# Router logits of an expert layer in four column tiles, summed by the matmuls that turn them

## The reference, cut to what matters

```python
x = hidden_states.reshape(-1, D)                     # 4096 x 512, after a layer norm
scores = jax.nn.softmax(x @ router_w, axis=-1)       # router_w is 512 x 8
topk_w, topk_idx = jax.lax.top_k(scores, TOP_K)      # 6 of 8 experts
g = jnp.einsum('td,edf->etf', x, w_gate)
u = jnp.einsum('td,edf->etf', x, w_up)
f_all = jnp.einsum('etf,efd->ted', jax.nn.silu(g) * u, w_down)
```

## Time and profile before

| | us |
|---|---|
| median of 3 executions | 2532.1 |
| fastest and slowest | 2517.46, 2537.41 |
| the profiled execution | 2517.62 |
| its span, first to last instruction | 2515.8 |
| mean granted TensorE clock, share of full | 0.973 |
| busy: TensorE matmuls, VectorE, ScalarE, GpSimd | 2391.5, 1376.7, 1181.9, 1334.4 |
| the logits' matmuls, L2354, busy | 22.8 + 7.5 |
| the transposes, L2362, busy | 2.6 |

### The profile page before, as it was taken

One profiled execution on the slowest core, in us unless ns is written; L12 is line 12 of the kernel. 1 busy time (PEld: TensorE's weight loads), 2 busy tenths in 40 slices (PEclk: granted clock), 3 DMA queues, 4 the chain that ended last, 5 costly groups with the idle time before them and its releaser, 6 DMA issues.

```text
span 2515.8 us, 34809 instructions
## 1 busy us (share of the span) xinstructions
PE 2391.5 (95%) x12552; PEld 1788.2 (71%) x12552; DVE 1376.7 (55%) x2160; ACT 1181.9 (47%) x2321; POOL 1334.4 (53%) x1415
## 2 busy tenths in 40 slices
PE   7999998999996999999789999999999999999998
PEld 6888884566665455554468877888777887788887
DVE  5555445777763455554554447544475444755544
ACT  3555566776731333333244435444354443544442
POOL 1444453433321122223477767777677776777773
PEclk9999997999996899999889999999999999999999
DMA  7655446666627344452322111321113211131120
GB/s 198 169 129 142 124 107 162 194 188 178 178 101 177 89 112 119 144 153 83 130 59 84 51 51 51 117 84 51 51 51 118 84 51 51 51 117 51 57 61 34
DMA packets 173963, 264.25 MB, mean 105 GB/s; under 512 B 13312, under 2 KB 100096, under 8 KB 165504
## 3 DMA queue, kind: packets, MB, share of 16 engines
q1 hardware_dynamic: 173536, 261.77, 36.7%
q10 hardware_dynamic: 256, 0.26, 0.0%
HBM read 167.55 MB, written 67.11 MB: 93 GB/s over the span
## 4 chain that ended last, share of the span: by engine, by line
PE 47%; DVE 2%; issue 1%; ACT 0%; POOL 0%; DVEq 0%; ACTq 0%
PE ex_pg L2381 30%; PE ex_pd L2397 17%; PE ex_pd L2354 1%; DVE ex_xb L2202 0%; DVE stage L2198 0%; DVE ex_ht L2231 0%; DVE ex_up L2222 0%; DVE ex_acc L2239 0%; ACT ex_xb L2047 0%; ACT ex_wg L2026 0%; DVE ex_h L2227 0%; ACT ex_m L2054 0%; DVE ex_t_a L2198 0%; PE ex_pd L2362 0%; DVE ex_t_b L2198 0%
## 5 line engine op out<-in xcount | busy, mean ns | idle before, releaser
L2381 PE MATMUL ex_pg<-ex_xb,ex_wg 128*128 128x512 f32 x3360 | 823.9, 392 | 17.0 <-DVE ex_up L2222 9.1
L2381 PEld LDWEIGHTS ex_pg<-ex_xb,ex_wg 128*128 128x128 f32 x3360 | 632.9, 189 | 159.3 <-issue 15.3
L2397 PE MATMUL ex_pd<-ex_wd,ex_ht 128*128 128x512 f32 x1920 | 486.4, 389 | 5.7 <-issue 5.7
L2397 PEld LDWEIGHTS ex_pd<-ex_wd,ex_ht 128*128 128x128 f32 x1920 | 360.1, 188 | 81.9 <-issue 7.3
L2239 DVE SCALAR_TENSOR_TENSOR ex_acc<-ex_pd,ex_share,ex_acc 128x512 f32<-128x512 f32 x320 | 239.6, 749 | 283.7 <-PE ex_pd L2397 283.2
L1986 POOL TENSOR_TENSOR ex_wg<-ex_sums,ex_wg 128x256 fp32r<-128x256 f32 x320 | 273.7, 871 | 112.8 <-ACT ex_wg L2026 112.8
L2054 ACT COPY ex_m<-ex_pg 128x512 f32<-128x512 f32 x240 | 140.8, 587 | 331.7 <-PE ex_pg L2381 331.5
L330 POOL TENSOR_TENSOR pr_ks_sum<-pr_ks_sum,pr_kp 128x512 f32<-128x512 f32 x128 | 165.1, 1291 | 160.8 <-DVE pr_kp L454 149.0
L2001 POOL TENSOR_TENSOR ex_h<-ex_g,ex_up 128x512 f32<-128x512 f32 x80 | 103.3, 1291 | 198.1 <-issue 195.1
L2058 ACT ACTIVATE ex_g<-ex_g 128x512 f32<-128x512 f32 x160 | 101.2, 633 | 187.5 <-DVE ex_g L2215 129.5
L541 PE MATMUL pr_pj<-pr_xt,pr_w 128*128 128x512 f32 x768 | 187.8, 400 | 1.4 <-DVE pr_xt L425 1.4
(11 more groups left out here) (192 smaller groups left out, 3700.6 us busy)
## 6 DMA issues: line engine op xcount, KB each, us to landing
stage<-in_units SPq DMA_DIRECT2D x120, 512.0 KB, 4.0
qk<-pr_kq SPq DMA_DIRECT2D x192, 128.0 KB, 2.4
qk<-q_scratch SPq DMA_DIRECT2D x96, 256.0 KB, 4.8
cr_q<-xq_scratch SPq DMA_DIRECT2D x96, 256.0 KB, 5.4
q_scratch<-pr_kq SPq DMA_DIRECT2D x128, 128.0 KB, 2.3
xq_scratch<-li_xq SPq DMA_DIRECT2D x32, 512.0 KB, 3.5
x_scratch<-cr_x SPq DMA_DIRECT2D x16, 1024.0 KB, 4.2
pr_x<-in_x SPq DMA_DIRECT2D x8, 1024.0 KB, 5.7
```

The costliest lines, as they stand in the source:

```text
L2381: mm = nc.tensor.matmul(pg[f][BANK[j]][:], wg[:, f, j, s, c * P:(c + 1) * P], xb[:, j, m, c * TB:(c + 1) * TB], start=(k == 0 and j in FRESH),
L2397: mm = nc.tensor.matmul(bank_of("D", n, i)[:], ht[:, s, f, k, t * P:(t + 1) * P], wd[:, n % 2, m, f * D:(f + 1) * D], start=(at == 0), sto ...
```

## The change

The four matmuls of a block of logits no longer accumulate into partitions 0 to 7. Each chunk c of D has its own strip of 32 partitions of the bank (c * HD, with HD = 32), and the stationary operand is widened from 8 to 32 columns of `r_raw`, whose columns behind the eighth are zeros. `lg` has 128 partitions in place of 8, and VectorE copies the whole bank. The transposes become plain fp32 matmuls with a 128 x 128 piece of `lg` as stationary operand and `pick` as the moving one, a 128 x 8 constant that is 1 where the partition modulo 32 is the expert: they turn the logits and add up the four strips. `pick` is a new input, loaded in SP's queue right behind the router's weights, and TensorE's first wait is for both.

```diff
+    pick = (np.arange(P)[:, None] % HD == np.arange(E)).astype(np.float32)
...
-        lg = sb("lg", [E, 2, TB])
+        lg = sb("lg", [P, 2, TB])
+        pick = sb("pick", [P, E])
...
                 sp.dma_start(r_raw[:], a["router"].rearrange("(c p) n -> p c n", p=P)).then_inc(const_in, 16)
+                sp.dma_start(pick[:], a["pick"]).then_inc(const_in, 16)
...
-                    nc.vector.tensor_copy(lg[:, k], bank_of("LG", half, k)[0:E, :]).then_inc(d_taken, 1)
+                    nc.vector.tensor_copy(lg[:, k], bank_of("LG", half, k)[:]).then_inc(d_taken, 1)
...
                     if half == 0:
-                        pe.wait_ge(const_in, 16)
+                        pe.wait_ge(const_in, 32)
                     bank_free("LG", half, k)
                     for c in range(C):
                         source = ((b11, b21), (b12, b22))[k][c // 2]
-                        mm = nc.tensor.matmul(bank_of("LG", half, k)[0:E, :], r_raw[:, c, 0:E],
-                                              source[:, c % 2 * TB:(c % 2 + 1) * TB], start=(c == 0), stop=(c == C - 1))
+                        mm = nc.tensor.matmul(bank_of("LG", half, k)[c * HD:(c + 1) * HD, :], r_raw[:, c, 0:HD],
+                                              source[:, c % 2 * TB:(c % 2 + 1) * TB], start=True, stop=True,
+                                              skip_group_check=True)
                     mm.then_inc(d_full, 1)
...
                     for n in range(NT):
-                        mm = nc.tensor.transpose(bank_of("LT", half, 0)[:, n * E:(n + 1) * E],
-                                                 lg[:, n // TT, n % TT * P:(n % TT + 1) * P], ident[0:E, 0:E])
+                        mm = nc.tensor.matmul(bank_of("LT", half, 0)[:, n * E:(n + 1) * E],
+                                              lg[:, n // TT, n % TT * P:(n % TT + 1) * P], pick[:], start=True, stop=True,
+                                              skip_group_check=True)
                     mm.then_inc(d_full, 1)
```

More of the change, by code:

```diff
@@ L94, in constants @@
         "ident": ident, "small": small, "one_col": one_col.reshape(P, -1), "rem_ones": rem_ones.reshape(P, -1),
-        "spread": spread.reshape(P, -1), "lower": lower.reshape(P, -1),
+        "spread": spread.reshape(P, -1), "lower": lower.reshape(P, -1), "pick": pick,
     }
```

## The result

The changed kernel ran 8 times, with a median of 2503.9 us (2501.83 to 2519.68), beside 8 runs of the kernel before with a median of 2525.3 us; one of these took 3031.4 us, and the median of the other seven is 2518.6 us. The ratio, without that run, is 0.9935, with a 95% interval of 0.9907 to 0.9963: faster by 0.65%, within 1% as forecast, clear of no change.

What follows compares the result with a forecast made beforehand. The expert stage was taken as one unbroken queue of TensorE matmuls away from its start. Three passes at 5.14 us gained less 1.4 us for the turn took 11.2 us off 2532.1: 2520.9 us, range 2504 to 2532.

Steps and rivals of the forecast that it cites:

- The logits: Logits of passes 2 to 4: four column tiles overlap completely, 6.97 us a pass becomes 1.83, gain 5.14 us.
- The turn: Transposes of the logits become 16 matmul records: 2.0 us in place of 0.58, cost +1.4 us a pass.
- The stall behind the turn: TensorE's 1.43 us wait before the down-projection, behind VectorE's ranking, moves with the turn and stays the same size: 0.
- Nothing else late: Around the logits, bank, GpSimd's split weights and VectorE's copy are ready though TensorE comes 5.14 us earlier: 0.
- The first pass: Start of the expert stage: TensorE waits 4.71 us for ScalarE's copy anyway, so earlier logits and dearer turn change nothing: 0.
- one cover: First pass: the last token part, delayed 0.4 to 0.5 us by pick's load, still lands before use; if not, 0.5 us.
- The sum: Three passes in the dense part, 3 x (5.14 - 1.4) = 11.2 us less; first pass 0.
- The level: Whole kernel: base is the three runs' median, 2532.1 us, giving 2520.9 us; range 2504 to 2532 us.
- The tiles do overlap: Rival on the logits, that tiles don't overlap here: only the turn's price is left, +4.2 us, 2536 us; chance 4%.
- came back as a wait: Rival behind the logits: TensorE arrives early and stands for GpSimd or ScalarE, 0 to +4 us; chance 6%.
- The slow side: Clock rival, expert stage's start: emptier TensorE stays at low clock longer, 2540 us; chance 5% for over 22 us.
- the stretch some 7 us longer: Milder clock case at the expert stage's start: +3.4 us, inside the range, as likely as not to happen.

Runs made afterwards that it cites:

- e6: Changed kernel with all four logits chunks accumulating in one 32-column strip and 32-row turn weights; 1227.13 us from step 1 to end, 2519.0 us in one run.
- e1: Changed kernel with the logits untiled (128x128 weights, accumulating) and the turn by pick kept; median 2523.8 us, ratio 1.0017 to the kernel before.
- e2: Changed kernel with two column strips of 64 in place of four of 32, each accumulating two chunks; median 2510.5 us, ratio 0.9984 to the kernel before.
- e3: Changed kernel with only the first pass's logits untiled; median 2504.8 us, ratio 0.9955 to the kernel before.
- e4: Changed kernel with VectorE's ranking of passes 2 to 4 moved behind the hidden state's low part; median 2497.3 us, ratio 0.9899 to the kernel before.
- e10: Changed kernel with ranking and third hidden low part moved later, pick loaded behind the last token part's; median 2493.4 us, ratio 0.9916 to the kernel before.
- e8: Changed kernel with VectorE's third hidden low part moved behind the second up product in every step; median 2500.2 us, ratio 0.9944 to the kernel before.

## Why the prediction was right

**The logits (5.14 us a pass): right.** They gave 5.12 us by the same distance, and 5.07 with the way in and out: 12.63 us from the product ahead of them to the down-projection behind them, and 1506.85 - 1499.29 = 7.56 after. The row of another stage with the same instruction shape carried the number: 0.86 us a group of eight records, and 1.83 us forecast against 1.85 measured. The Trainium skill's lower packing factor ("TensorE: Matmul & The Clock Gate", packing small matmuls), 3.07 for four row tiles and from it an estimated 4.7 us, did not hold for these column tiles: e6 to the changed kernel is 6.98 to 1.85 us, a factor of 3.8 with the way out included.

**The turn (+1.4 us): too high.** It cost 1.12 us by the same distance. By the whole step 7 it cost 1.03 (33.74 - 37.78 = -5.07 + 1.03), because the transposes' 8-row weights had held up their own start by 0.09 us: 1508.08 - 1506.63 = 1.45 us behind the product's start in the kernel before, 1517.73 - 1516.37 = 1.36 after. 1.70 us for 16 records are 0.106 us each, the lower end of the 0.109 to 0.136 I read from the earlier trace rows. The distance from first matmul to the next line's was the right reading; the 1.09 us of weight loads held a first load that ran beside the matmuls before it. The Trainium skill's rule for a weight load (same page, LDWEIGHTS: 107 ns for 128 columns) gives 1.7 us, and the trace agrees.

**The stall behind the turn (0): nearly.** It moved with the turn, but is 0.24 us shorter in all three passes. Most of that is VectorE's subtraction in the chain, which took 0.34 us in place of 0.77. In the kernel before it ran from 1509.29 us on beside one of GpSimd's sums (1509.23 to 1509.97 us), after the change it began 0.25 us before such a sum ended. e1 and e2 have the shorter stall too (1.21 us), so it comes with the turn and not with the tiles.

**Nothing else late (0): right.** No wait stands behind the logits in TensorE's waits, and steps 9, 19 and 29 are unchanged. But the view of the stage that this rested on, one unbroken queue of matmuls away from its start, was wrong: besides the 1.43 us stalls, the kernel before has a wait of 0.71 to 0.74 us in each of steps 8, 18 and 28, and two of 0.49 to 1.48 us in each of steps 10, 20 and 30. They are the same after the change, so the forecast did not suffer by it.

**The first pass (0): right**, by the unchanged 20.2 us to ScalarE's copy, and by e3. But one cover was thinner than I had said. The last token part was used 5.8 us after its issue and TensorE's wait for it ended 5.1 us after it (1263.11 - 1258.00), so it was 0.7 us early, where I had read 3 us from the router's weights. I priced a load of 512 KB by the landing of the router's weights, half its size.

**The sum: -11.2 us forecast, -12.75 measured.** The difference is 3 x 0.28 from the turn and 3 x 0.24 from the stall.

**The level: off.** 2520.9 us was forecast and 2503.9 measured, 0.1 us below the low edge of the range (2504). The term that was mis-sized is the base, by more than the whole gain: I took the median of three runs, 2532.1 us, of which two lay 15 to 20 us above the third. These two have no trace; that the stretch in the projections was at half clock in them is inferred. Of 19 later runs of the kernel before the median is 2517.8 us, and 2517.8 - 12.75 = 2505. The profiled run at the low end was the sign I had in hand, and I had used it for the range's end alone. The traced gain of 12.75 us is 0.51% of the span, inside the interval of the measured ratio.

**The rivals.** The tiles do overlap (e2, e6). Nothing of the gain came back as a wait. The slow side came in part and cost nothing. Up to step 1 the changed kernel was granted 0.50 in 29.3 us (1257.1 to 1266.2, 1273.2 to 1286.7 and 1290.2 to 1296.9), the kernel before in 22.8 us (1242.3 to 1248.1, 1261.8 to 1272.0 and 1275.4 to 1282.2). That is the stretch some 7 us longer, priced at 3.4 us; but what was added lay ahead of ScalarE's copy, for which TensorE waits anyway, and step 1 came only 0.05 us later. The dense part is at full clock.

The time to step 1 varies more, from 45.24 to 49.27 us over twelve kernels, and e3 and e1 execute the same in the first pass and took 49.27 and 46.91 us. Their stretches from 16 to 41 us of the stage, columns as in the earlier trace rows, e3 first:

```profile
1257.55:1282.55 25.00, 16.06 (x49) 12.16 (x49) 14.43 (x17) 13.27 (x26) 20.21 (x24) 0.66 0.23 64
1273.18:1298.18 25.00, 16.47 (x67) 12.92 (x66) 15.03 (x20) 15.91 (x29) 20.32 (x23) 0.86 0.22 64
```

The time goes with this granted clock. With an untiled first pass it is 0.66 in the four kernels that took 48.91 to 49.27 us and 0.86 in e1 and e6 (46.91 and 46.84 us); with a tiled one it is 0.59 in the four that took 48.95 to 49.03 us, 0.66 in e4 (47.66) and 0.80 in e10 (45.24). So e10's early step 1 is no gain of its edits that these runs show. Why the clock rises sooner in some executions stays open. So does what sets the 37 us stretch in the projections: five of the twelve profiles have it, and their expert stages begin at 1257.0 to 1263.7 us, those of the other seven at 1241.5 to 1243.2.

## What to carry to other kernels

When a stage is one queue of matmuls, price an edit by the distance between starts in rows of the same instruction shape, wherever in the kernel these stand: here that was within 0.02 us. Before comparing two executions, cut their spans at the first instruction that the change can touch, since a stretch at half clock ahead of it was larger than the change. And ask of every wait in a summary in which steps it lies: the stalls behind the router's ranking, hidden in a total, were worth 7.3 us for one moved call, more than half of what the tiles brought.

## What the runs showed of the hardware

Narrow weights cost something even without tiles beside them: 16 untiled plain fp32 records with 8 or 32 columns, together with the products around them, took 12.63 and 12.65 us, with 128 columns 12.31 us (the kernel before, e6, e1). The Trainium skill ("TensorEngine Tiling (Array Packing)", Key Properties) says that a change of tiling mode drains TensorE; the 0.3 us a pass agree with that, though no run isolates the drain. The kernel before paid them already with its 8 columns, so that the tiles added none of their own.

A subtraction on VectorE with two operands in SBUF took 0.68 us alone and 1.70 to 1.84 us while GpSimd split weights. The Trainium skill ("SBUF — State Buffer", the two separate sides) says that such an instruction and one of GpSimd lock a shared pair of ports for each other in full. The rows agree: in the changed kernel GpSimd's pair of instructions ends at 1533.65 us and VectorE's at 1534.20. In step 7 of the changed kernel the two meet the other way round:

```profile
1495.04 3.00 POOL L1996 TENSOR_TENSOR ex_wd<-stage,ex_wd 128x512 fp32r<-128x512 f32 x2
1496.07 0.82 DVE L2234 TENSOR_TENSOR ex_ht<-ex_h,ex_ht 128x512 fp32r<-128x512 f32 x1
```

VectorE's instruction begins before GpSimd's second one and takes only 0.82 us, and GpSimd's pair takes 3.00 us in place of 2.54. In these rows the one that begins later is the one that is held. e8 shows that the place of the instruction decides whether TensorE waits; the lock itself no run has isolated.
